# Conditional residual kernel, one core: chunks 6 and 7 turned amid z, x of slot 0 on ACT's DMA queue and turned fourth, last slot's end in quarters

## The reference

```python
x = x + einsum('bct,bcd->bdt', x, weights[itok_B_0_15])     # 16 matrices of 64 x 64
x = x + einsum('bsi,boi->bso', x, weight[itok_B_3_7])       # 8 adapters of 1024 x 1024
```

## Time and profile before

| what | value |
|---|---|
| median of 3 runs | 796.29 us (796.24 to 798.08) |
| profiled execution, its own time | 796.8 us |
| its span, first to last instruction | 795.1 us |
| mean granted TensorE clock | 0.998 |
| PE busy | 778.8 us, 98% of the span |
| DVE, ACT, POOL busy | 590.6, 457.1, 254.5 us |
| HBM read and written | 57.15 MB and 33.55 MB |

### The profile page before, as it was taken

The page is one execution under the profiler, slowest core; times in us unless marked ns, Lnnn a source line. Parts: engine busy times, 40 slices in busy tenths (PEclk is TensorE's granted clock), DMA queues, the critical chain, the costliest instruction groups (busy, mean ns, idle before and its releaser), DMA issues.

```text
span 795.1 us, 19206 instructions
## 1 busy us (share of the span) xinstructions
PE 778.8 (98%) x3448; PEld 645.2 (81%) x3449; DVE 590.6 (74%) x706; ACT 457.1 (57%) x772; POOL 254.5 (32%) x158
## 2 busy tenths in 40 slices
PE   5999999999999999999999999999999999999996
PEld 5788888888888888888888888888888888888885
DVE  7688887788887567888876788887576756756765
ACT  3465566557656555665655566556554654654554
POOL 2444533253452212435421243452122122122110
PEclk9999999999999999999999999999999999999999
DMA  8334443444442333454333444432332233233233
GB/s 264 96 108 147 144 141 107 137 130 126 148 120 65 106 100 119 122 146 145 96 102 106 123 125 136 155 101 86 106 98 77 75 106 90 68 106 99 62 104 80
DMA packets 73955, 90.89 MB, mean 114 GB/s; under 512 B 13781, under 2 KB 64470, under 8 KB 73942
## 3 DMA queue, kind: packets, MB, share of 16 engines
q1 hardware_dynamic: 63574, 57.97, 24.0%
q10 hardware_dynamic: 10368, 32.78, 14.3%
HBM read 57.15 MB, written 33.55 MB: 114 GB/s over the span
## 4 chain that ended last, share of the span: by engine, by line
PE 96%; DMA 1%; DVE 1%; issue 0%; POOL 0%; ACT 0%; ACTq 0%; SPq 0%; DVEq 0%; POOLq 0%
PE z_ps L544 15%; PE z_ps L545 15%; PE first_ps L544 15%; PE first_ps L545 15%; PE z_ps L547 15%; PE first_ps L547 13%; PE y_ps L557 7%; DMA w_nat<-in_L_cond_weight_dram 1%; DVE y L927 0%; PE y_ps L525 0%; PE first_ps L525 0%; DVE z_parts L920 0%; ACT y L669 0%; POOL w_nat L315 0%; ACTq L215 0%
## 5 line engine op out<-in xcount | busy, mean ns | idle before, releaser
L356 POOL TENSOR_TENSOR xt_lo<-x_turned,xt_hi 128x1024 fp32r<-128x1024 f32 x61 | 146.7, 2405 | 249.9 <-ACT xt_hi L653 248.4
L544 PE MATMUL z_ps<-w_hi,xt_hi 128*128 (+1 forms) x528 | 205.8, 390 | 0.0
L544 PE MATMUL first_ps<-w_hi,xt_hi 128*128 x528 | 205.5, 389 | 0.0
L545 PE MATMUL z_ps<-w_lo,xt_hi 128*128 (+1 forms) x528 | 205.4, 389 | 0.0
L545 PE MATMUL first_ps<-w_lo,xt_hi 128*128 x528 | 205.4, 389 | 0.0
L927 DVE TENSOR_TENSOR y<-y_ps,y 64x512 f32<-64x512 f32 x254 | 174.6, 689 | 33.6 <-ACT y L669 27.7
L547 PE MATMUL z_ps<-w_hi,xt_lo 128*128 (+1 forms) x512 | 199.2, 389 | 0.0
L547 PE MATMUL first_ps<-w_hi,xt_lo 128*128 x480 | 186.7, 389 | 0.0
L669 ACT ACTIVATE y<-y_ps 64x512 f32<-64x512 f32 x254 | 150.5, 594 | 11.3 <-issue 2.2
L658 ACT ACTIVATE z_parts<-z_ps 64x512 fp32r<-64x512 f32 x132 | 78.5, 595 | 132.6 <-PE y_ps L557 93.4
L658 ACT ACTIVATE z_parts<-first_ps 64x512 fp32r<-64x512 f32 x132 | 78.5, 595 | 131.4 <-PE y_ps L557 103.6
(11 more groups left out here) (135 smaller groups left out, 360.0 us busy)
## 6 DMA issues: line engine op xcount, KB each, us to landing
x_in<-in_x_dram SPq DMA_DIRECT2D x536, 64.0 KB, 2.4
out_dram<-y ACTq DMA_DIRECT2D x124, 256.0 KB, 3.6
w_nat<-in_L_cond_weight_dram SPq DMA_DIRECT2D x128, 128.0 KB
w_nat<-in_L_cond_weight_dram SPq DMA_DIRECT2D x4, 512.0 KB, 6.6
y<-in_L_cond_weight_dram SPq DMA_DIRECT2D x2, 512.0 KB, 7.1
w_turned<-in_L_cond_weights_dram SPq DMA_DIRECT2D x2, 256.0 KB, 3.8
x_in<-in_x_dram SPq DMA_DIRECT2D x2, 256.0 KB, 4.6
x_turned<-in_L_cond_weight_dram SPq DMA_DIRECT2D x1, 512.0 KB, 5.3
```

The lines of the kernel that those rows point to most:

```text
L356: nc.gpsimd.tensor_tensor(xt_lo[h][:], x_turned[h][:], xt_hi[h][:].bitcast(F32), ALU.subtract).then_inc(xt_lo_made, 1)
L544: nc.tensor.matmul(to, xt_hi[h][:, t, :], whi, start=(t == 0), stop=False)
L545: mm = nc.tensor.matmul(to, xt_hi[h][:, t, :], wlo, start=False, stop=last and not pair)
```

## The change

Four edits, of which two go together:

1. SP issues all eight chunks one behind the other. The two samples of slot 0 are issued by ACT on its own queue, when DVE has found them, ahead of ACT's first copy. In `TURN_ORDER` x of slot 0 moves from third place to fourth.
2. PE turns chunks 6 and 7 after the first four tiles of z's half 0 instead of ahead of them (`LAST_TURNS`). POOL adds 1 to chunks 6 and 7 right behind chunk 5, ahead of the six small operations of the group table, and DVE's three increments that stand for slot 0 come ahead of the table instead of behind it.
3. The last slot's second z half is made in two quarters of 256 columns, all 8 tiles each, in different banks; y of half 0 comes behind the first quarter, y of the first quarter ahead of the second quarter's last tile.
4. In the last slot y is made by twice as many matmuls, of 64 output rows each, that add up in PSUM, so that ACT (sample 0) and DVE (sample 1) only copy it. Each sample's last rows leave in three DMAs instead of two.

```diff
-        TURN_ORDER = [0, 1, X0, 2, 3, 4, 5, 6, 7]
+        TURN_ORDER = [0, 1, 2, X0, 3, 4, 5, 6, 7]
+        LAST_TURNS = 2
...
+        last_z_banks = [z_banks[1][0], z_banks[1][1], z_banks[1][0]]
+        LAST_COLUMNS = [slice(0, HALF), slice(HALF, HALF + HALF // 2), slice(HALF + HALF // 2, T)]
...
@@ tensor
             def first_half(pair):
                 pe.wait_ge(first_lo_made, NH * FOR_FIRST_HALF)
-                sum_z(0, 0, 0, pair)
+                sum_z(0, 0, 0, pair, range(0, KT // 2))
+                for i in range(len(TURN_ORDER) - LAST_TURNS, len(TURN_ORDER)):
+                    turn_first(i)
+                sum_z(0, 0, 0, pair, range(KT // 2, KT))
...
+            def sum_last_y(part, pair):
+                for k in range(2):
+                    pe.wait_ge(w0_placed, 2 * s + k + 1)
+                    pe.wait_ge(z_lo_made, PER_Z * s + 2 * part + k + 1)
+                    own = k if pair else 0
+                    for w in range(2):
+                        mm = nc.tensor.matmul(last_y_banks[part][own][rows_of(0), LAST_IN_BANK[part]],
+                                              w0_parts[:, k, w * C:(w + 1) * C],
+                                              z_parts[:, min(part, 1), k, LAST_IN_HALF[part]],
+                                              start=w == 0 and (pair or k == 0), stop=w == 1 and (pair or k == 1))
+                    mm.then_inc(y_summed, 1)
...
             def last_half(pair):
-                sum_z(1, 1, buf, pair, range(0, KT // 2))
-                sum_y(s, pair, last_y_banks, (0,))
-                sum_z(1, 1, buf, pair, range(KT // 2, KT))
+                sum_last_z(1, pair)
+                sum_last_y(0, pair)
+                sum_last_z(2, pair, range(0, KT - 1))
                 pe.wait_ge(y_made, PER_Y * (2 * pairs_past) + (PER_Y + MADE_AHEAD))
-                sum_y(s, pair, last_y_banks, (1,))
+                sum_last_y(1, pair)
+                sum_last_z(2, pair, range(KT - 1, KT))
+                sum_last_y(2, pair)
@@ scalar, behind it: act and dve take the last slot part by part
+            begin_half_y(0)
+            keep_last_z_hi(1)
+            begin_half_y(1)
+            take_last_y(0)
+            take_last_y(1)
+            keep_last_z_hi(2)
+            take_last_y(2)
+            store_last(act, 1, sample, stores)
```

More of the change, by code:

```diff
@@ L197, in conditional_residual_kernel @@
         y_made = sem("y_made")
+        last_made = [sem(f"last_made{k}") for k in range(2)]
         last_stored = sem("last_stored")
@@ L319, in _ @@
                 add_1_to_first(c)
-            for c in range(4, 6):
+            for c in range(4, CHUNKS_PER_GROUP):
                 add_1_to_first(c)
@@ L413, in load_first @@
                              ).then_inc(first_loaded[c], 16)
[L415 to L424, removed]
+            for c in range(CHUNKS_PER_GROUP):
                 load_first(c)
@@ L549, in sum_z, with sum_y @@
                     mm.then_inc(z_summed, 1)
-            def sum_y(s, pair, banks=y_ps, halves=range(NH)):
-                for n in halves:
+            def sum_y(s, pair):
+                for n in range(NH):
                     for k in range(2):
@@ L699, in rest_of_slot @@
                 store_y(act, before, 1 - h)
+            act.wait_ge(samples_made, 1)
+            _, first_samples = nc.values_load_multi_w_load_instructions(
+                first_samples_i[:], engines=[act.engine], min_val=0, max_val=B - 1,
+                skip_runtime_bounds_check_because="the table is made on the chip, of clipped indices")
+            for k, sample in enumerate(first_samples):
+                act.dma_start(x_in[0][k * C:(k + 1) * C, :], x_rows[bass.ds(sample * C, C), :]).then_inc(x0_loaded, 16)
             for i in range(len(TURN_ORDER)):
@@ new lines, in _, with keep_last_z_hi, take_last_y @@
+            act.wait_ge(y_summed, PER_Y * before + 4)
+            place_w0(s)
+            def keep_last_z_hi(part):
+                act.wait_ge(z_summed, NH * s + part + 1)
+                for k in range(2):
+                    nc.scalar.activation(z_parts[rows_of(k), 1, k, LAST_IN_HALF[part]],
+                                         last_z_banks[part][rows_of(k), LAST_IN_BANK[part]], ACT.Copy).then_inc(z_hi_made, 1)
+            def take_last_y(part):
+                with act.If(stores > 1):
+                    act.wait_ge(y_summed, PER_Y * s + 2 * part + 1)
+                    nc.scalar.activation(y[1][rows_of(0), LAST_COLUMNS[part]],
+                                         last_y_banks[part][0][rows_of(0), LAST_IN_BANK[part]],
+                                         ACT.Copy).then_inc(last_made[0], 1)
+                with act.Else():
+                    act.wait_ge(y_summed, PER_Y * s + 2 * part + 2)
+                    nc.scalar.activation(y[1][rows_of(0), LAST_COLUMNS[part]],
+                                         last_y_banks[part][0][rows_of(0), LAST_IN_BANK[part]],
+                                         ACT.Copy).then_inc(last_made[0], 1)
```

120 lines of the change are left out of this document (74 added, 46 removed).

## The result

The changed kernel is slower: median 804.13 us (803.51 to 805.04, 5 runs) against 796.38 (796.24 to 798.08, 5 runs) for the kernel before, ratio 1.0093, 95% interval 1.0082 to 1.0104, so 7.7 us, or 0.9%. The forecast was 795.2 within 793.2 to 797.8. The profiled execution took 804.06 us, its span is 802.3 (before 795.1), and PE is busy for 781.3 us of it.

A forecast was written before the change was run, and what follows sets the result against it. PE was taken as the bound, busy 778.8 of 795.1 us. Beginning -0.95 + 0.65 = -0.3 and end 1.7 - 2.5 = -0.8 gave -1.1 us: 795.2 against the median, range 793.2 to 797.8.

The forecast's parts named there:

- The beginning, x on ACT's queue: Beginning: x delays chunk 1 on the full DMA engines, so z begins 0.65 us later, bounds 0 and +3.0.
- in them nothing changes: Beginning: from slot 1's last rest to the end of xt_lo stays 6.58 us (table, turn of x, ACT, POOL).
- z ahead of chunks 6 and 7: Beginning: z can begin at 20.5 and slot 1 at 33.8, xt_lo ending 0.2 behind PE; gain 0.95 us.
- z by quarters: End: 256-column matmuls and doubled y matmuls make z end later by 52 p - 5.05, 1.7 us.
- p: End: time from start to start of a matmul with 256 columns, taken as 0.13 us.
- the slower rival: End: 256-column matmuls stay at 0.23 us, weight loads not hidden; end +4.4, total 800.4 us; chance 0.1.
- the chain: End: from z's end to the end of the span, 5.2 us instead of 7.72; saves 2.5, between 1.8 and 2.8.
- the shared queue costs most: Beginning: rival, chunk 1 comes 2 us or more late and PE's turns stay slow; +1.2, 797.5 us; chance 0.2.

The follow-up runs named there:

- low16_after: The changed kernel, reading group and chunk numbers from the low 16 bits of their table words: 804.77 us, ratio 1.0092 to the kernel before.
- low16_x_sp: The changed kernel with low-16-bit table reads, x of slot 0 issued by SP as before but still turned fourth: 800.38 us, ratio 1.0039.
- low16_amid_sp3: The changed kernel with low-16-bit table reads, x of slot 0 issued by SP and turned third as before: 796.71 us, ratio 1.0005.
- low16_x_act: The kernel before with low-16-bit table reads and x of slot 0 issued by ACT, still turned third: 800.81 us, ratio 1.0049.
- low16_best_early: The changed kernel, low-16-bit reads, x on SP turned third, POOL waiting for the table, last DMAs issued once their rows are made: 796.39 us, ratio 0.9988.
- ctl_after: The changed kernel with range assertions on the group number and chunk bounds read from the table: 806.79 us, ratio 1.0127.
- x_sp: The changed kernel with range assertions on table reads, x of slot 0 issued by SP but still turned fourth: 804.13 us, ratio 1.0086.

## Why the prediction was wrong

**Step "The beginning, x on ACT's queue": this failed.** I wrote that x would share the DMA engines with chunk 1, that chunk 1 would come 0.6 to 1.2 late, and took +0.65 with +3.0 as the bound. With x on ACT's queue chunk 1 was late in no profile (POOL takes it by 11.1), and x was the one that was late, by 5.7 us (landed 19.2 instead of 13.5). The term is for z's beginning, which moved from 23.72 only to 24.20 because the turns of chunks 6 and 7 were moved behind it as well; by the prediction's own 20.5 without the delay, z came 3.7 late. I had costed who loses when two queues share, and picked the wrong one; the row that warned was the earlier trace rows, 209 GB/s at a full share while 64-row DMAs ran. I took that as a property of x for 2.5 us at most, and it held for 5 us over all that ran beside it. Measured: +4.4 us (low16_after less low16_x_sp; 2.7 with assertions), +3.7 alone, where 0.65 was forecast and 3.0 the bound.

**Edit "x fourth".** I gave the new place no cost of its own. With x on SP it leaves PE waiting 1.22 us for chunk 2 with x's turn still to come. low16_x_sp to low16_amid_sp3 is 3.7 us, but that is from a kernel whose profile has DVE held to one most of whose executions are fast. Against the three high executions of low16_amid_sp3 (798.79 to 800.5) low16_x_sp is -0.1 to +1.6: so I estimate the place itself at 1.6 at most, and no run separates it.

**Step "in them nothing changes" (table, turn of x, ACT, POOL), 6.58 us.** This failed too: 39.33 - 30.81 = 8.52 us. The edit moves DVE's table operations and POOL's small matrices onto the same moment. I had asked whether POOL would be late for xt_lo, not whether it would hold DVE, though my own times had POOL's operation begin at 30.4 - 2.4 = 28.0 and DVE's table operations right behind the last rest at 27.2, less than a microsecond apart. The late x has a part in it too: in low16_x_act the two meet with the chunks turned as before. Its 1.9 us and the slow pace behind the wait are worth 3.65 us in the changed kernel.

**Step "z ahead of chunks 6 and 7": right in mechanism and size.** With x third on SP and the meeting taken away, z begins at 20.34, slot 1 at 34.01 behind a wait of 0.68 for xt_lo (low16_best_early); I had 20.5, 33.8 and 0.2 at undisturbed turns. xt_lo does bind, as said. In time the better beginning gives 0.6 to 1.2, where I had 0.95.

**Step "z by quarters": right in p, and in the sum partly by luck.** The matmuls are 0.12 apart, against p = 0.13, and z ends 1.8 later (8.6 us behind the last slot's first y, against 6.8), forecast 1.7. But 52 x 0.12 - 5.05 is 1.2 only. Most of the rest is PE standing idle for some 0.5 us ahead of y of the first quarter (0.35 of it for DVE), a wait that the sum had at nothing. A weight load of the same 128 columns hides behind 256: the slower rival is excluded.

**Step "the chain", 7.72 to 5.2: the arithmetic held, the issues did not.** The copies are done 2.44 us behind z. I wrote that the DMA issues "just fit, since two of them go out while PE and DVE work"; in the code all three stand behind ACT's last copy, SP's three stand behind its read of the table, and where they were moved the last DMA itself took up to 4.1 us, not 2.55 to the end. Measured 7.1, which is 1.9 more than forecast; the end costs +0.4 by the medians (within their noise; 0.7 and 1.2 in the profiles) instead of -0.8. Why it stays at 7.0 with early issues is open.

The rival "the shared queue costs most" had the right edit and the wrong victim, and priced it at +1.2.

## What to carry to other kernels

Ahead of a second DMA queue ask which transfer loses, and look at the rate while narrow transfers run: here they took it from everything beside them, with the engines at a full share. When an edit moves an operation, list what the other engines do at its new time, DVE's operations with two inputs in SBUF and GpSimd's above all, and not only who waits for it. A chain ends with its DMA issues and their landing: read in the code where each issue stands.

## What the hardware showed that I had not expected

Two DMAs of 64 rows on a second queue brought the rate from some 400 to 225 to 266 GB/s for 5 us and landed 9.6 us after issue (9.2 to 10.4 in the other such kernels). On the chunks' own queue the rate fell to 209 as well, but only for some 2 us, and they took 4.6 (3.8 to 5.1). One DMA of 128 rows on the second queue left the rate at 406 to 422 and took 8.4. A DVE operation on 69 numbers took 2.17 instead of 0.28 us beside a GpSimd operation. A wait of PE of 2.45 to 2.67 us ahead of slot 1 was followed by a granted clock of 0.50 for about 3 us in five kernels (the change, ctl_after, low16_after, low16_x_sp and low16_amid_sp3), but not in x_sp, where it stayed at 1.00 behind a wait of 2.53; behind a wait of 0.66 to 0.68 it never fell. The turns of the first chunks have the slow pace (1.97 us for eight, against 1.06 later) while the granted clock reads 1.00.
